# Causal attention on one core: denominators from summed key-major weights, scores in rounded 32-bit halves with two heads in the array's row halves

## The reference, cut to what matters

```python
Q = split_heads(x)                       # B=8, S=1024, 16 heads of 16
K = split_heads(x @ Wk + bk)
V = split_heads(x @ Wv + bv)             # 16 heads of 64
scores = einsum('bhqd,bhkd->bhqk', Q, K) + causal_mask      # float32, no scale
attn = softmax(scores);  o = einsum('bhqk,bhkd->bhqd', attn, V)
x1 = layernorm(x + (x + gelu(o) @ Wf + bf))
gate, up = x1 @ wg.T, x1 @ wu.T          # 256 -> 768, int weights / 127
out = layernorm(x1 + (silu(gate) * up) @ wd.T)
```

## Time and profile before

| | us |
|---|---|
| median of 3 runs | 2221.79 (2221.63 to 2221.82) |
| span of the profiled execution, first to last instruction | 2219.1 |
| stage B, PE's first scores to the last copy of `o_acc` | about 1636 |
| stage C | about 522 |
| busy: PE / ACT / DVE / POOL | 94% / 77% / 61% / 26% |

### The profile page before, as it was taken

The page is one execution under the profiler, slowest core; times in us unless marked ns, Lnnn a source line. Parts: engine busy times, 40 slices in busy tenths (PEclk is TensorE's granted clock), DMA queues, the critical chain, the costliest instruction groups (busy, mean ns, idle before and its releaser), DMA issues. The chain is left out here.

```text
span 2219.1 us, 43484 instructions
## 1 busy us (share of the span) xinstructions
PE 2080.9 (94%) x10816; PEld 1069.3 (48%) x10816; DVE 1364.0 (61%) x2593; ACT 1701.5 (77%) x4083; POOL 574.2 (26%) x1258
## 2 busy tenths in 40 slices
PE   5699999999999999999999999999989999999996
PEld 4343344333433344333433334322224888888885
DVE  6667667666767667666767667655541455545554
ACT  0599898988989888988989889988885655555553
POOL 3123232222313232222323132211121221222212
PEclk9799999999999999999999999999999999999998
DMA  6534343525344343424344343422231223332310
GB/s 214 144 113 125 106 138 87 153 77 150 88 131 124 106 134 91 147 83 145 89 135 124 106 129 97 143 79 68 78 132 72 87 87 113 113 104 72 108 67 20
DMA packets 271245, 242.95 MB, mean 109 GB/s; under 512 B 42896, under 2 KB 217104, under 8 KB 271120
## 3 DMA queue, kind: packets, MB, share of 16 engines
q1 hardware_dynamic: 271120, 241.66, 36.4%
HBM read 139.86 MB, written 101.71 MB: 109 GB/s over the span
## 5 line engine op out<-in xcount | busy, mean ns | idle before, releaser
L1010 DVE TENSOR_REDUCE negmax<-scores 128x1 f32<-128x128 f32 (+7 forms) x1024 | 771.4, 754 | 429.9 <-PE scores L574 426.3
L823 ACT ACTIVATE scrap<-scores,negmax 128x128 bf16<-128x128 f32 (+7 forms) x1024 | 770.7, 753 | 105.1 <-DVE negmax L1010 92.6
L834 ACT ACTIVATE weights<-scoresT 128x512 f32<-128x512 f32 (+3 forms) x1536 | 705.2, 502 | 137.7 <-PE scoresT L574 132.7
L574 PE MATMUL o_acc<-weights,v_pair 128*64 128x512 f32 (+3 forms) x3072 | 676.7, 520 | 0.0
L543 POOL TENSOR_SCALAR_AFFINE_SELECT weights<-weights 128x128 f32<-128x128 f32 x1024 | 319.0, 312 | 1155.6 <-ACT weights L834 1152.0
L574 PE MATMUL scores<-k_stack,q_stack 96*128 96x512 bf16 (+3 forms) x1536 | 436.6, 340 | 75.2 <-ACT scrap L823 61.0
L574 PE MATMUL scoresT<-q_stack,k_stack 99*128 99x512 bf16 (+3 forms) x1536 | 457.7, 333 | 26.5 <-ACT weights L834 4.4
L574 PEld LDWEIGHTS scores<-k_stack,q_stack 96*128 96x128 bf16 x1536 | 112.6, 98 | 614.3 <-ACT scrap L823 349.7
L574 PEld LDWEIGHTS o_acc<-weights,v_pair 128*64 128x64 f32 x3072 | 153.6, 136 | 170.3 <-issue 147.1
L574 PE MATMUL scores<-wf_sb,g 128*128 128x256 f32 x1024 | 229.4, 380 | 1.6 <-DVE y_pre L1066 0.8
L574 PE MATMUL scores<-causal,ident 128*128 128x128 bf16 x1024 | 229.6, 224 | 0.0
(11 more groups left out here) (114 smaller groups left out, 1920.4 us busy)
## 6 DMA issues: line engine op xcount, KB each, us to landing
v_pairs<-v_unit SPq DMA_DIRECT2D x64, 512.0 KB, 4.7
v_pair<-v_pairs SPq DMA_DIRECT2D x64, 512.0 KB, 4.5
o_heads<-o_pair SPq DMA_DIRECT2D x64, 512.0 KB, 3.2
g<-o_heads SPq DMA_DIRECT2D x16, 2048.0 KB, 8.1
q_stack<-q_parts SPq DMA_DIRECT2D x384, 64.0 KB, 2.2
k_stack<-k_parts SPq DMA_DIRECT2D x384, 64.0 KB, 2.2
q_parts<-q_split SPq DMA_DIRECT2D x48, 256.0 KB, 2.6
k_parts<-k_split SPq DMA_DIRECT2D x48, 256.0 KB, 4.2
```

Source lines behind the costliest of these rows:

```text
L574: return nc.tensor.matmul(o, l, r, start=start, stop=stop)
L823: nc.scalar.activation(scrap[h][:, 0:width], sc[h][:, 0:width], ACT.Exp, bias=negmax[r % 2][:, slot], accum_out=den[r % 2][:, slot]).then_ ...
L834: nc.scalar.activation(weights(h, u, c0, c1), st[c % 2][:, 0:c1 - c0], ACT.Exp).then_inc(s_w, 1)
L1010: v.tensor_reduce(negmax[r % 2][:, slot:slot + 1], sc[h][:, 0:P * (ORDER[u] + 1)], AX.X, ALU.max, negate=True).then_inc(s_max, 1)
```

## The change

- **Operands.** q and k are no longer three bf16 parts but the two rounded 32-bit halves that stage A has anyway (`x_hi`, `x_lo`, `k_hi`, `k_lo`), 48 rows a head: hi·hi, hi·lo, lo·hi. One head lies in rows 0 to 49 of `q_stack`, the other in rows 64 to 113, and a matmul for each is issued back to back, to two banks. The splitting of q and k by DVE and POOL goes. A pair's stacks load in 4 DMAs instead of 12.
- **Scores.** They are made in 12 blocks a pair of at most 512 keys, both heads a block. The mask matmul goes; where a block holds the diagonal, and in the second blocks, DVE adds the mask inside the max (`tensor_tensor_reduce`, one a head, 16 a pair); four blocks a pair take a plain max of both heads. ACT's exponential over these scores, its sum and the logarithm go.
- **Key-major weights.** `scoresT` is now both heads at once, up to 2 x 512, in one buffer of two banks. ACT's 12 exponentials a pair are up to 1024 wide. The shift is the maximum alone, two rows. They are made 20 blocks behind the scores (`DELAY`).
- **Denominators.** POOL (10 instructions) and DVE (2) add the 12 weight tiles of a pair into sums over the key tiles; four float32 matmuls with a matrix of ones (`denominators`) sum over the partitions; ACT copies the result out, and SP stores it. Every four pairs a small load, a DVE reciprocal and a store follow.
- **Copies.** ACT instead of DVE copies `o_acc` and V out of PSUM. K is read twice by DVE.
- **Stage C.** The attention output is not normalised yet. Per unit SP loads the reciprocals spread over 64 partitions each (`den_wide`, 2 DMAs, 2 MB written), and POOL multiplies `g` by them (`norm`, 8 instructions of 128 x 512) before ACT's gelu.

The core of the diff (PE, ACT, POOL):

```diff
-                if place > 0 or r > 0:
-                    pe.wait_ge(s_den, 2 * NT * n + 2 * place + h - 1)
-                mm(sc[h][:, width - P:width], ident16[:], causal[:], False, True).then_inc(s_sc, 1)
+                if r > 0 or j >= 2:
+                    pe.wait_ge(s_max, NS * n + j - 1)
+                for h in range(2):
+                    rows = slice(HSTEP * h, HSTEP * h + SROWS)
+                    e = mm(sc[j % 2][:, h, 0:w], q[rows, P * u:P * (u + 1)], k[rows, BANK * kc:BANK * kc + w],
+                           True, True)
+                e.then_inc(s_sc, 1)
...
-                    if r > 0 or c >= 2:
-                        pe.wait_ge(s_w, PER_ST * n + c - 1)
-                    mm(st[c % 2][:, 0:c1 - c0], k[:, h, P * u:P * (u + 1)], q[:, h, c0:c1],
-                       True, True).then_inc(s_st, 1)
+                if rt > 0 or t > 0:
+                    pe.wait_ge(s_w, NS * n + t)
+                for h in range(2):
+                    rows = slice(HSTEP * h, HSTEP * h + SROWS + SHROWS)
+                    e = mm(st[:, h, 0:width_of(t)], k[rows, P * u:P * (u + 1)],
+                           q[rows, q0_of(t):q0_of(t) + width_of(t)], True, True)
+                e.then_inc(s_st, 1)
...
+            def denominators(rn, n):
+                pe.wait_ge(s_oev, 2 * (n + 1))
+                pe.wait_ge(s_add, NA * (n + 1))
+                for h in range(2):
+                    for c in range(2):
+                        row = SQ * (2 * h + c)
+                        e = mm(oo[1][row:row + SQ, :], ones[:], (acc0[rn % 2] if c == 0 else acc1)[:, h, :], True, True)
+                e.then_inc(s_den, 1)
...
+                for j in range(NS):
+                    back, t = after(r, j, DELAY)
+                    if 0 <= back < PAIRS:
+                        scoreT(t, back, n + back - r, it)
+                    if r < PAIRS:
+                        score(j, r, n, it)
+                    back, t = after(r, j, DELAY + BEHIND)
+                    if 0 <= back < PAIRS:
+                        weigh(t, r, back, n + back - r, it)
+                    back, t = after(r, j, DELAY + DEN_AT)
+                    if 0 <= back < PAIRS and t == 0:
+                        denominators(back, n + back - r)
+                    job_beside(r, it, j)
...
-                            nc.scalar.activation(scrap[h][:, 0:width], sc[h][:, 0:width], ACT.Exp,
-                                                 bias=negmax[r % 2][:, slot], accum_out=den[r % 2][:, slot]
-                                                 ).then_inc(s_den, 1)
+                nc.scalar.activation(W[t][:, :, :], st[:, :, 0:width_of(t)], ACT.Exp).then_inc(s_w, 1)
...
+            def norm(r, it):
+                n = r + 2 * it
+                for c in range(HC):
+                    if c == 0:
+                        pool.wait_ge(s_dn, 32 * (n + 1))
+                    pool.wait_ge(s_g[r % 2], 16 * (r // 2 + it + 1))
+                    pool.tensor_tensor(g[r % 2][:, c], g[r % 2][:, c], dn[:, c], ALU.mult).then_inc(s_gn, 1)
...
             def finish(r, it):
+                if r + 1 < UNITS:
+                    norm(r + 1, it)
                 if r >= 1:
                     m = r - 1 + 2 * it
...
+            def load_dn(r, it):
+                b, t0 = unit_of(r, it)
+                n = r + 2 * it
+                if r >= 1:
+                    sp.wait_ge(s_gn, HC * n)
+                    settle(sp, s_passed["sp"])
+                for h in range(2):
+                    sp.dma_start(dn[DV * h:DV * (h + 1)], rd[bass.ds(b, 1), h:H:2, t0:t0 + U].rearrange(
+                        "o c t -> (o c) t").partition_broadcast(DV)).then_inc(s_dn, 16)
```

More of the change, by code:

```diff
@@ L53 @@
 QSCALE = 1.0 / 127.0
+HSTEP = 64
+SROWS = 48
+SHROWS = 2
+GT = tuple((0, u) for u in range(4)) + tuple((1, u) for u in range(8))
+GS = ((2, 0), (3, 0), (0, 0), (1, 0), (4, 0), (5, 0), (6, 0), (7, 0), (4, 1), (5, 1), (6, 1), (7, 1))
+NS = 12
+DELAY = 20
+BEHIND = 3
+O0_AT = 7
+O1_AT = 15
+DEN_AT = 17
+ALONE = 2
+JOB_SLOTS = (4, 6, 8)
 def walk(eng, steps, first, unroll, rounds, body):
@@ L799, in _, with copy_v @@
             act.preload_act_table_set(LN_EXP)
+            def copy_v(j, a, bank, first=False):
+                what, i, hf = JOBS[j]
+                act.wait_ge(s_job, NJ * a + j + 1)
+                if not first and hf == 0:
+                    act.wait_ge(s_vst[i], 16 * a)
+                copy(vs[:, i, BANK * hf:BANK * (hf + 1)], bank).then_inc(s_ev, 1)
+            for a in range(ALONE):
+                for j in range(DC, NJ):
+                    copy_v(j, a, a_banks[(NJ * a + j) % NB], a == 0)
@@ new lines, in attend @@
+                for j in range(NS):
+                    back, t = after(r, j, DELAY)
+                    if 0 <= back < PAIRS:
+                        exponent(t, back, n + back - r)
+                    back, t = after(r, j, DELAY + O0_AT)
+                    if 0 <= back < PAIRS and t == 0:
+                        copy_o(0, back, n + back - r, it)
+                    back, t = after(r, j, DELAY + O1_AT)
+                    if 0 <= back < PAIRS and t == 0:
+                        copy_o(1, back, n + back - r, it)
+                    back, t = after(r, j, DELAY + DEN_AT + 1)
+                    if 0 <= back < PAIRS and t == 0:
+                        copy_den(back, n + back - r, it)
+                    i = job_at(r, it, j - 1)
+                    if i is not None and i >= DC:
+                        copy_v(i, unit_beside(r, it), oo[0][:])
@@ L1002, in attend, with carry_sum, reciprocals @@
+            def carry_sum(n):
+                dve.wait_ge(s_w, NS * n + 7)
+                dve.wait_ge(s_add1, 2 * n + 1)
+                v.tensor_tensor(acc1[:], acc1[:], W[6][:], ALU.add).then_inc(s_add1, 1)
+            def reciprocals(i, first):
+                dve.wait_ge(s_dcl, 16 * (i + 1))
+                if not first:
+                    dve.wait_ge(s_rst, 16 * i)
+                v.reciprocal(den_r[:], den_c[:]).then_inc(s_rec, 1)
             def attend(r, it):
```

771 lines of the change are left out of this document (386 added, 385 removed).

## The result

The changed kernel takes 2520.95 us (median of four runs, 2518.13 to 2523.05) against 2221.71 for the kernel before on the same chip. The ratio is 1.1349, 95% interval 1.1334 to 1.1364. The prediction was 2465 with a range of 2290 to 2640.

What follows compares the result with a forecast made beforehand. ACT with its handshakes sets stage B and PE sets stage C in the kernel before. 2221.8 + 73 (stage B) + 170 (stage C) = 2465 us, range 2290 to 2640.

Steps and rivals of the forecast that it cites:

- Direction and cause: Whole kernel 11% slower; in stage C POOL's `norm` waits for `den_wide`, making `h_lo` late and PE stand 9.5 us.
- ACT, DVE, POOL in stage B: Stage B work per pair: ACT 12.9 us, DVE 17.2, POOL 16.6, none of them a bound.
- The rival of a doubled max: Stage B: the masked max costs double, DVE has 25.0 us of work a pair; total 2530 us, chance 0.10.
- The loop and the path: Stage B: each block takes the larger of `scoresT`-exponential loop (1.83 us at 512) and PE's path (1.75); 21.0 a pair.
- the first stretch of the loop: Stage B, block of 512: weight load 0.19, streaming 0.21, result 0.17, ACT start 0.12 us.
- The shift's wait: Stage B: for one pair in four the shift stands on SP behind `store_v`; 0.3 us a pair.
- The clock: Stage B: PE streams less, so the granted clock dips, also beside jobs; 1.5 us a pair, between nothing and 2.5.
- Stage B in sum: 26.8 us a pair with jobs, 22.8 without; stage B 1709 us against 1636, +73.
- Its sign of being wrong: The forecast is wrong if a pair takes under 22.9 us, or if stores of z stay 31 us apart.
- Stage C: Late `den_wide` and `norm` cost 11.5 us a unit, 150 over 13 units, plus 20 at the start: +170 us.
- store plus `den_wide` are the same 2.5 MB, so they land at about Z + 9.7: Stage C: `den_wide` lands 9.7 us after the store of z (Z), priced by the loads of `g` and the 0.5 MB behind.
- My upper bound of 200 for stage C: Stage C loses at most 200 us, if the 64-fold spreading reads slower than `g`; the lower bound was 110.

Runs made afterwards that it cites:

- e4_no_norm: The changed kernel without POOL's products with the denominators' reciprocals and without the loads of `den_wide`, leaving out part of the computation: 2259.35 us, 1.017.
- e2_dn_early: The changed kernel with SP's loads of `den_wide` in stage C issued one turn earlier, ahead of the wait for z: 2362.28 us, 1.0621.
- e1_shift_first: The changed kernel with SP moving the shift rows ahead of the stores of attention output, q, k and V: 2388.94 us, 1.0762.
- e8_one_half: e7_dve_norm with both heads' scores and `scoresT` made from the first row half, the second head's scores left out: 2606.99 us median.
- e3_both: The changed kernel with both the edits of e1_shift_first and e2_dn_early: 2231.59 us, 1.0055.
- e9_one_load: The changed kernel with `den_wide` filled from distinct attention output rows in one transfer over 128 partitions, without the division by denominators: 2429.66 us, 1.0935.
- e7_dve_norm: e3_both with the eight products of `g` and `den_wide` per unit made by DVE instead of POOL: 2186.28 us, 0.9855.

## Why the prediction came out right, and where it did not

**Direction and cause** hold: in stage C POOL's queue holds `norm` ahead of `h_lo`, and the late `den_wide` makes PE wait. e4_no_norm and e2_dn_early show it. Stage C carries 266 of the 299 us.

**ACT, DVE, POOL in stage B.** Predicted 12.9, 17.2 and 16.6 us a pair with jobs. The stretch of 1320 us holds 50.8 pairs of 26.0: 12.2, 16.7 and 15.8. The masked max, for which no row existed, takes 685 ns at 512 columns, as the stand-in of 692 said. With a second operand it takes 737, and reading its result takes 81 more each. The rival of a doubled max falls.

**The loop and the path.** Predicted 1.83 and 1.75 us for a block of 512; measured 1.62 and about 1.67 (0.67 from `scoresT` to the product behind a score of 512, and 1.0 of product). The step that failed is the first stretch of the loop, 0.69 of load, stream, result and start, where the trace has 0.54, and 0.62 in the pairs with jobs, whose blocks take 1.70. So an undisturbed pair was 21.0 and 25.0 in the prediction, and is 20.5 without jobs and 23.6 with them in e1_shift_first. This made the prediction 1.4 us too slow for a pair with jobs: 0.5 for the blocks, and 0.9 for the jobs, which add 3.1 in place of 4.0.

**The shift's wait.** Predicted 0.3 us a pair; PE's waits are 91.9 us, and in four pairs with jobs 2.4 and 4.2, so 1.7 a pair. That is the worst-sized term of stage B. I had seen the transfer behind `store_v`, but counted its wait as one pair in four. It strikes two of four, and each time the two trips of the shift, out and in, come on top.

**The clock.** Predicted 1.5 us a pair, from PE streaming less, and in the pairs without jobs too. With jobs the dips come with the waits for shifts and go with them (e1_shift_first). They cost about 0.7 a pair, what is left of 2.4 when the waits' 1.7 are taken off, while e8_one_half, where PE is busier, has the most of them. There the term was twice too large, and its reason was wrong. The pairs without jobs ran at 1.00 from 1480 to 1680 us in this profile, but not in each: e3_both is at the lower level for 31 us between 1400 and 1458, with no PE wait over 1.5 us. For these pairs the reason stays open.

**Stage B in sum** came out as 26.0 us a pair for 26.8 and 20.5 for 22.8, and +32 us for +73, with the 11 ahead of stage B in it, for which the prediction had no term. The closeness of the pair is luck: loop, path and jobs too long by 1.4, shifts and clock too short by 0.6 (1.8 for the 2.4 that e1_shift_first takes away). Its sign of being wrong, a pair under 22.9 us, is met by the pairs without jobs and by one in four of the others (22.7), though not by their mean; and the clock of 0.9 or less in stage B did not come (0.94 and 1.00). One aside of the working does not add up: with 24.0 a pair its own terms give -79, not -60; and 1655.2 less 82.7 us are 63 steps of 64 shifts. With e1_shift_first stage B ends at 1594 us, 101 before the kernel before, and a pair with jobs takes 23.6; the relief of ACT is real, and SP's order hid it.

**Stage C.** Per unit +11.5 was predicted and +18 measured. In the unit above:

| from the store of z | predicted | measured |
|---|---|---|
| `den_wide` there | 9.7 | 15.6 |
| eight products | 9.1 | 9.8 |
| PE resumes | 20.8 | 27.35 |
| PE resumes to next store of z, over before | 2.0 | 2.8 |

The step that failed is "store plus `den_wide` are the same 2.5 MB, so they land at about Z + 9.7": bytes alone do not set it. e9_one_load, where the load has g's shape, gives 8.6 us and 43.4 us a unit; the prediction's unit was 42.6. Thirteen units by 5.9 us are 77 us, more than the 56 by which the whole forecast is short. The longer start of stage C was +20 predicted, +31 measured, with the same load in it: the first `h_lo` comes 61 us after stage B's end, not 51. My upper bound of 200 for stage C did not hold the 266; it allowed for the spreading of a row, which costs 1 us, and not for the width of the transfer.

**Range.** 2290 to 2640 held the time, since stage B's overshoot of 41 us made up for part of stage C's 96.

## What to carry to other kernels

Where work leaves the engine that bounds a stage, look first at the queues that the new work is put into: here two edits of SP's order took 289 us away, nearly all of the 299 that the change had cost. Price a transfer by a row with the same number of partitions on both ends and the same outer dimension, not by bytes alone: the same 2 MB took 8.6 us in one piece, 12.3 in two halves, or about 43 with two rows as the outer dimension. When a load is moved ahead, look at what now stands behind it, as `g` does here. Before two rows of waits are added, see whether they are one wait, as PE's and PEld's are. And before work is put on POOL beside DVE, ask what both do in SBUF at that time, since each of DVE's operations may last as long as POOL's.

## What was not expected of the hardware

- Two products in the two row halves start 3 ns apart and cost as one. In one half they start 335 ns apart, a pair takes 29.7 us in the mean for 23.6, and the clock falls to 0.89 where it was 0.99, though PE is the busier one.
- Two transfers of 64 partitions land in 12.3 us, one of 128 with the same bytes in 8.6, with the DMA engines as busy in both. Eight whose source has two rows run at 49 GB/s with a tenth of the DMA engines.
- DVE's `tensor_scalar` of 256 columns takes 407 ns, and 1081 to 1208 beside POOL's products; DVE's product of 512 columns 0.69 us, and 1.34 beside POOL's `h_lo`.
- An activation of 128 columns lasts 0.28 us in its record but holds the next one back by 0.17 to 0.18.
- What is left open: the third of e7_dve_norm's 3.2 us a unit that PE's wait for `hidden` does not cover, whether loading `g` ahead of `den_wide` wins the rest, and what brings the clock down in e8_one_half and in the pairs without jobs.
